# A new front for the scan layer of a two-layer perceiver kernel: input blocks in the cross-attention, step sizes by a stacked rounded product, first taps on ScalarE, other banks for folds

## The reference, cut to what matters

```python
def _L0_attn_ref(x, ...):                     # x: 16 x 64 x 256, after a layernorm
    x_b, res = split(x @ in_proj_w.T + in_proj_b, 2)          # 512 channels each
    xc = depthwise_conv(x_b, conv_w, 4 taps, causal) + conv_b
    x_b = silu(xc)
    delta, b, c = split(x_b @ x_proj_w.T, [16, 32])           # 16 + 16 + 16 columns
    delta = softplus(delta @ dt_proj_w.T + dt_proj_b)
    a = -exp(A_log)
    h = exp(delta * a) * h + delta * b * x_b  # 64 steps in time, 16 states a channel
    y = sum over states(h * c) + x_b * D_param
    return (y * silu(res)) @ out_proj_w.T + out_proj_b
```

## Time and profile before

| | us |
|---|---|
| median of 3 runs | 684.99 |
| lowest and highest | 683.14, 686.74 |
| the profiled execution | 687.29 |
| its span on the core | 685.6 |
| TensorE busy | 619.4 |
| VectorE busy | 471.8 |
| ScalarE busy | 366.0 |
| GpSimd busy | 223.2 |

### The profile page before, as it was taken

How to read it: one execution, slowest core, us unless ns; L and a number is a source line. 1 busy time by engine, 2 the same in 40 slices (tenths; PEclk the granted TensorE clock), 3 DMA queues, 4 the chain that set the end, 5 groups by cost and what they waited for, 6 DMA issues and landing times. The chain is left out here.

```text
span 685.6 us, 11634 instructions
## 1 busy us (share of the span) xinstructions
PE 619.4 (90%) x4414; PEld 461.1 (67%) x4414; DVE 471.8 (69%) x804; ACT 366.0 (53%) x679; POOL 223.2 (33%) x180
## 2 busy tenths in 40 slices
PE   3998999998998777887878899999999999999997
PEld 2453555554335666776767888887877767889897
DVE  5122333345857989999999746678987778777554
ACT  2310111123549898999999742433566456455342
POOL 2000000000003999999989200034553021232000
PEclk9998999999999999999999999999999999999999
DMA  8999999882821232232331000000100022120000
GB/s 309 394 336 420 418 420 419 319 316 77 231 83 43 74 108 98 93 120 97 106 111 62 1 1 1 16 1 17 34 3 3 1 63 77 47 62 1 32 1 32
DMA packets 31071, 86.48 MB, mean 126 GB/s; under 512 B 7900, under 2 KB 19576, under 8 KB 28840
## 3 DMA queue, kind: packets, MB, share of 16 engines
q1 hardware_dynamic: 30456, 85.28, 34.3%
q10 hardware_dynamic: 560, 0.46, 0.3%
HBM read 83.50 MB, written 1.11 MB: 123 GB/s over the span
## 5 line engine op out<-in xcount | busy, mean ns | idle before, releaser
L692 POOL TENSOR_TENSOR dbu<-du,bs 128x1024 f32<-128x1024 f32 x63 | 148.8, 2414 | 212.3 <-DVE du L884 209.5
L906 DVE TENSOR_TENSOR_SCAN w_in<-hS,dbu 128x1024 f32<-128x1024 f32 x42 | 94.7, 2273 | 0.1
L784 ACT ACTIVATE weighed<-T,CT 128x256 f32<-128x256 f32 x220 | 90.8, 536 | 3.4 <-PE T L988 3.1
L773 ACT ACTIVATE hS<-delta,negA 128x504 f32<-128x504 f32 x128 | 86.9, 751 | 7.6 <-DVE xn L906 5.4
L1002 PE MATMUL Y<-ident,weighed 128*128 128x128 f32 x512 | 67.7, 275 | 0.1
L988 PE MATMUL T<-ident,w_in 128*128 128x128 f32 x336 | 46.6, 282 | 22.3 <-ACT weighed L784 13.6
L1002 PEld LDWEIGHTS Y<-ident,weighed 128*128 128x128 f32 x512 | 58.7, 142 | 0.8 <-DVE sres L927 0.3
L988 PEld LDWEIGHTS T<-ident,w_in 128*128 128x128 f32 x336 | 36.7, 142 | 32.7 <-DVE w_in L906 30.7
L906 DVE TENSOR_TENSOR_SCAN xn<-hS,dbu 128x1024 f32<-128x1024 f32 x22 | 50.1, 2278 | 5.6 <-issue 4.7
L258 PE MATMUL S<-cT,qkT 128*64 128x512 f32 (+1 forms) x256 | 47.7, 527 | 2.8 <-DMA cT<-in_ctxT 2.8
L270 PE MATMUL O<-cN,pT 128*64 128x256 f32 x384 | 46.7, 385 | 0.0
(11 more groups left out here) (416 smaller groups left out, 1315.9 us busy)
## 6 DMA issues: line engine op xcount, KB each, us to landing
cT<-in_ctxT SPq DMA_DIRECT2D x8, 3202.0 KB, 15.5
cN<-in_ctx SPq DMA_DIRECT2D x8, 3072.0 KB, 14.4
bs<-b_rows SPq DMA_DIRECT2D x32, 512.0 KB, 3.5
raw_w<-in_w SPq DMA_DIRECT2D x16, 256.0 KB, 2.8
w<-in_w SPq DMA_DIRECT2D x7, 256.0 KB, 8.3
vs<-vx SPq DMA_DIRECT2D x8, 136.0 KB, 2.3
x<-in_x SPq DMA_DIRECT2D x2, 512.0 KB, 6.0
cR<-in_ctx SPq DMA_DIRECT2D x1, 1024.0 KB, 32.3
```

Of the source, the lines that this page charges most:

```text
L692: e.tensor_tensor(dbu[s % NB][:, :, :], half(m.du, s // DS), row, ALU.mult).then_inc(s_bu, 1)
L773: i = e.activation(by_batch(A[s % 2][:, j * HALF:(j + 1) * HALF]), by_batch(m.delta[:, c, h * HALF:(h + 1) * HALF]), ACT.Exp, scale=m.negA ...
L784: i = e.activation(weighed[s % 2][:, q * Q:(q + 1) * Q], T[:, q * Q:(q + 1) * Q], ACT.Copy, scale=c_of(s, q))
L906: e.tensor_tensor_scan(S[s % NS], A[s % 2][:, :], dbu[s % NB][:, :, :].rearrange("p c n -> p (c n)"), 0.0, ALU.mult, ALU.add).then_inc(s_h, 1)
```

## The change

- The cross-attention's end makes four input blocks, not one. Block 0 stands ahead of the last fold of `on`, block 1 ahead of the last output projection, 2 and 3 around the last two folds of normed tokens. ScalarE moves all four out there.
- The first tap is ScalarE's (`first_tap`), into four buffers and not two; VectorE does three taps.
- `x_proj` writes 128 rows: the 16 rows of delta three times (rows 0, 32, 64) and b and c at 96. ScalarE rounds 80 of them to fp32r (`large_part`), VectorE writes what the rounding left to rows 32 on (`small_part`). The weights are prepared alike by GpSimd (`w_dt3`), so that one product of 80 rows of rounded operands gives the three larger terms. Four banks serve for it, not two.
- GpSimd, idle in the front before, copies `w_xp`'s columns, prepares `w_dt3` and adds the output bias `outb` to `k.x` (128x2048), which VectorE did in the last step.
- Softplus goes in three parts: the first two channel blocks before `absolute` 3 to 7, the others on ScalarE after the first decays. Max(z, 0) plus logarithm of the second half moves from GpSimd to VectorE (steps 2 and 3), those of blocks 1 to 3 of the first half to GpSimd.
- The products of layer 1's weights use Y where they used A; ScalarE copies their results out, after the decays of step 2. TensorE makes D times u for the first unit after the first fold, and step 1 isn't weighed by VectorE any more, nor step 0.
- b goes to memory and back for each half by itself. `w_dt` is loaded three times; two clears at the program's start grow, and `own_head`, which nothing read, goes.

```diff
-    def begin_scan_layer():
-        e.wait_ge(k.s_wi, 16)
-        e.wait_ge(s_xT, 2)
-        project_in(e, k, 0, bank[2]).then_inc(s_in, 1)
+    def begin_scan_layer(n):
+
+        if n == 0:
+            e.wait_ge(k.s_wi, 16)
+            e.wait_ge(s_xT, 2)
+        project_in(e, k, n, bank[(n + 2) % 4]).then_inc(s_in, 1)
...
                 turn(i - 1, g)
+        if i > TILES:
+            begin_scan_layer(0)
         if i >= 2:
             weighted(i - 2)
+        if i > TILES:
+            begin_scan_layer(1)
...
-    begin_scan_layer()
+    begin_scan_layer(2)
     turn_normed(2)
+    begin_scan_layer(3)
     turn_normed(3)
...
+    def keep_block(n):
+
+        e.wait_ge(s_in, n + 1)
+        if n < 2:
+            e.wait_ge(s_tn, n + 1)
+        e.activation(xb(k, n), bank[(n + 2) % 4], ACT.Identity, bias=col(k, "inb", n)).then_inc(s_xb, 1)
+
+    keep_block(0)
+    keep_block(1)
     root(2)
-    e.wait_ge(s_in, 1)
-    e.wait_ge(s_tn, 2)
-    e.activation(xb(k, 0), bank[2], ACT.Identity, bias=col(k, "inb", 0)).then_inc(s_xb, 1)
-    for n in (2, 3):
-        move_normed(n)
+    keep_block(2)
+    move_normed(2)
+    keep_block(3)
+    move_normed(3)
...
+with ExitStack() as front:
+    sbf, _, _ = tools(nc, front)
+    dtr3 = sbf("dtr3", [DT_ROWS, TOK], F32R)
+    w_dt3 = sbf("w_dt3", [DT_ROWS, DI], F32R)
...
-acc4 = [weighed[1][:, r * HALF:(r + 1) * HALF].rearrange("p (b l) -> p b l", l=L) for r in range(2)]
+acc4 = [weighed[r // 2][:, r % 2 * HALF:(r % 2 + 1) * HALF].rearrange("p (b l) -> p b l", l=L) for r in range(4)]
...
-kTb = dbu[2][:, :, :].rearrange("p c n -> p (c n)")[:, 0:KD * (D + 1)].rearrange("p (c n) -> p c n", c=KD)
-qk, qk_at = A[1].rearrange("p (j n) -> p j n", j=KD), HALF // 2 + 8
+kTb = k.xz[:, :, :].rearrange("p c n -> p (c n)")[:, 0:KD * (D + 1)].rearrange("p (c n) -> p c n", c=KD)
+qk, qk_at = Y.rearrange("p (j n) -> p j n", j=KD), HALF // 2 + 8
-xq, dq = ([a[:, i * HALF:(i + 1) * HALF] for i in range(2)] for a in A)
+xq = [a[:, 0:HALF] for a in A]
+dq = [A[i % 2][:, (1 - i // 2) * HALF:(2 - i // 2) * HALF] for i in range(4)]
...
-    return s % 16 in (0, 1, 3, 5, 7, 9, 11, 13, 15)
+    return s > 1 and s % 16 in (0, 1, 3, 5, 7, 9, 11, 13, 15)
...
+    e.wait_ge(k.s_w2, k.n_w2)
+    for r in DT_AT[1:]:
+        i = e.tensor_copy(k.w_xp[:, :, r:r + DTR], k.w_xp[:, :, 0:DTR])
+    i.then_inc(s_ws, 1)
+    e.tensor_copy(w_dt3[:, :], k.w_dt[0:DT_ROWS, :]).then_inc(s_ws, 1)
+    e.wait_ge(s_ws, 2)
+    low = slice(DT_AT[2], DT_ROWS)
+    e.tensor_tensor(w_dt3[low, :], k.w_dt[low, :], w_dt3[low, :].bitcast(F32), ALU.subtract).then_inc(s_ws, 1)
+    e.wait_ge(s_ws, 3)
+    e.wait_ge(k.s_rows, 16)
+    e.tensor_tensor(k.x[:, :, :], k.x[:, :, :],
+                    rowvec(k, "outb").unsqueeze(1).to_broadcast([P, TILES, D]), ALU.add).then_inc(s_xo, 1)
     for s in range(1, STEPS):
-        if s in (3, 6):
-            steps_by_input(0, s // 3 + 1)
-        if s in (9, 12, 21, 24):
-            add_parts((9, 12, 21, 24).index(s))
-        if s in (15, 18, 34, 37):
-            steps_by_input(1, (15, 18, 34, 37).index(s))
         if s == 1:
-            e.wait_ge(s_du, 2)
+            add_parts(1)
+            steps_by_input(0, 1)
+        if s in (4, 8):
+            add_parts(2 + (s - 4) // 4)
+        if s in (6, 10):
+            steps_by_input(0, 2 + (s - 6) // 4)
+        if s in (18, 22, 26, 30):
+            steps_by_input(1, (18, 22, 26, 30).index(s))
+        if s == 1:
+            e.wait_ge(s_du, 1)
+            e.wait_ge(s_dup, 2)
+            e.wait_ge(s_fp, pe_at["dt", 7])
...
+    def first_tap(n):
+
+        c = n % CH
+        if n >= CH:
+            e.wait_ge(s_fa, ac_at["xb", n])
+            e.wait_ge(s_fa, ac_at["u", n - 4])
+        e.activation(acc4[n % 4][:, :, :], xb(k, n).rearrange("p (b l) -> p b l", l=L), ACT.Identity,
+                     scale=col(k, "convw", c * KC + KC - 1), bias=col(k, "convb", c)).then_inc(s_fa, 1)
...
+    def large_part(h):
+
+        e.wait_ge(s_fp, pe_at["xj", h])
+        e.activation(dtr3[:, h * HALF:(h + 1) * HALF], xq[h][0:DT_ROWS, :], ACT.Copy).then_inc(s_fa, 1)
...
+    parts = (halves[0][:, 0:2, :], halves[0][:, 2:4, :], halves[1])
+
+    def exponential(g):
+        e.wait_ge(s_fa, ac_at["abs", (1, 3, 7)[g]])
+        e.activation(parts[g], parts[g], ACT.Exp, scale=-1.0).then_inc(s_fa, 1)
+
+    def logarithm(g):
+        e.wait_ge(s_fa, ac_at["exp", g])
+        e.activation(parts[g], parts[g], ACT.Ln, bias=1.0).then_inc(s_fa, 1)
+
+    first_tap(0)
+    first_tap(1)
+    keep_block(4)
+    first_tap(2)
     silu_u(0)
...
+    for n in range(3):
+        absolute(n)
+    large_part(1)
+    keep_rows(1)
+    e.preload_act_table_set("natural_log_exp_and_others")
+    exponential(0)
+    logarithm(0)
+    for n in range(3, 2 * CH):
+        absolute(n)
-    e.activation(m.delta[:, :, :], m.delta[:, :, :], ACT.Exp, scale=-1.0).then_inc(s_fa, 1)
-    e.wait_ge(s_fa, ac_at["exp", 0])
-    for part in (halves[0][:, 0:2, :], halves[0][:, 2:4, :], halves[1]):
-        e.activation(part, part, ACT.Ln, bias=1.0).then_inc(s_fa, 1)
+    e.wait_ge(s_fa, ac_at["exp", 3])
     e.mul(m.negA[:, :, :].rearrange("p c n -> p (c n)"), expA[:, :], -1.0).then_inc(s_fa, 1)
...
     decays(0)
+    e.wait_ge(s_fp, pe_at["vo", 0])
+    e.activation(vT, T[:, HALF:2 * HALF], ACT.Copy).then_inc(s_vo, 1)
+    exponential(1)
+    exponential(2)
+    decays(1)
+    logarithm(1)
+    logarithm(2)
+    decays(2)
+    e.wait_ge(s_fp, pe_at["b", 0])
+    e.activation(k.w5[0][:, :, :], qk[:, :, 0:D], ACT.Copy)
+    e.activation(k.w5v[:, :, D + 2], qk[:, :, D], ACT.Copy)
+    e.activation(k.bq5[:, :], Y[:, qk_at:qk_at + KD], ACT.Copy)
+    e.activation(k.btq[:, 2:3], Y[:, qk_at + KD:qk_at + KD + 1], ACT.Copy).then_inc(s_qt, 1)
     e.wait_ge(s_fp, pe_at["vo", 1])
     e.activation(k.wfq[0:1, :], spare[0:1, 0:D], ACT.Copy)
     e.activation(k.w5v[:, :, 0:D], T[:, HALF:2 * HALF].rearrange("p (c n) -> p c n", c=KD), ACT.Copy).then_inc(s_vo, 1)
-    decays(1)
     e.wait_ge(s_ct, 1)
     for s in range(STEPS):
-        if s + 2 < STEPS:
+        if 0 < s < STEPS - 2:
             decays(s + 2)
...
-        if n:
-            e.wait_ge(s_fa, ac_at["xb", n])
-        if n >= 2:
-            e.wait_ge(s_fa, ac_at["u", n - 2])
-        for j in range(KC):
+        e.wait_ge(s_fa, ac_at["tap", n])
+        for j in range(1, KC):
             tap = col(k, "convw", c * KC + KC - 1 - j)
-            if j == 0:
-                e.tensor_scalar(acc4[r][:, :, :], x, tap, col(k, "convb", c), ALU.mult, ALU.add).then_inc(s_cv, 1)
-            else:
-                e.wait_ge(s_cv, 4 * n + j)
-                e.scalar_tensor_tensor(acc4[r][:, :, j:L], x[:, :, 0:L - j], tap, acc4[r][:, :, j:L],
-                                       ALU.mult, ALU.add).then_inc(s_cv, 1)
-
-    def keep_rows(h):
+            if j > 1:
+                e.wait_ge(s_cv, 3 * n + j - 1)
+            e.scalar_tensor_tensor(acc4[r][:, :, j:L], x[:, :, 0:L - j], tap, acc4[r][:, :, j:L],
+                                   ALU.mult, ALU.add).then_inc(s_cv, 1)
+    def small_part(h):
+
         hs = slice(h * HALF, (h + 1) * HALF)
-        e.wait_ge(s_fp, pe_at["xj", h])
-        e.tensor_copy(dtr[:, hs], xq[h][0:DTR, :])
-        e.tensor_copy(m.bc[32:64, hs], xq[h][32:64, :]).then_inc(s_xe, 1)
+        at = slice(DT_AT[1], DT_AT[1] + DTR)
+        e.wait_ge(s_fa, ac_at["hi", h])
+        e.tensor_tensor(dtr3[at, hs], xq[h][at, :], dtr3[at, hs].bitcast(F32), ALU.subtract).then_inc(s_lo, 1)
...
-    for n in range(6):
+    for n in range(7):
         convolve(n)
-    keep_rows(0)
-    convolve(6)
-    positive(0)
-    positive(1)
+    small_part(0)
     convolve(7)
-    positive(2)
-    positive(3)
-    keep_rows(1)
     for c in range(CH):
         i = e.tensor_scalar(m.diagD[:, c, :], k.ident[:, :], col(k, "dpar", c), None, ALU.mult)
     i.then_inc(s_dg, 1)
-    for n in range(CH, 2 * CH):
+    for n in range(3):
         positive(n)
+    small_part(1)
...
-    e.tensor_copy(CT[:, :, :], T[:, 0:TILES * 2 * DS].rearrange("p (t n) -> p t n", n=2 * DS)).then_inc(s_ct, 1)
-    for c in range(2):
-        add_parts(c)
-    for c in range(2):
-        e.wait_ge(s_dl, c + 1)
-        e.tensor_tensor(m.du[:, c, 0:HALF], m.delta[:, c, 0:HALF], m.u[:, c, 0:HALF], ALU.mult).then_inc(s_du, 1)
-    e.wait_ge(s_du, 2)
+    e.tensor_copy(kTb[:, :, 0:D], Y[:, HALF:2 * HALF].rearrange("p (c n) -> p c n", c=KD)).then_inc(s_qt, 1)
+    positive(3)
+    raw_gate(6)
+    positive(4)
+    add_parts(0, 0)
+    e.wait_ge(s_dl, 1)
+    e.tensor_tensor(m.du[:, 0, 0:HALF], m.delta[:, 0, 0:HALF], m.u[:, 0, 0:HALF], ALU.mult).then_inc(s_du, 1)
+    for n in range(5, 2 * CH):
+        positive(n)
+    for r in range(2):
+        e.wait_ge(s_fa, ac_at["abs", 2 * CH - 2 + r])
+        e.wait_ge(s_rz, 2 * CH - 1 + r)
+        zeros(r)
+    e.wait_ge(s_fp, pe_at["dt", 7])
+    e.wait_ge(s_du, 1)
+    e.wait_ge(s_dup, 2)
```

(65 more changed lines are left out.)

174 lines of the change are left out of this document (84 added, 90 removed).

## The result

The kernel before took 684.65 us (median of 7 runs, 683.1 to 686.8), the changed kernel 690.32 (7 runs, 689.2 to 692.9). The ratio is 1.0096, with a 95% interval of 1.0076 to 1.0117: 0.96% slower. The forecast was 690.4. One execution of a kernel of experiment 10 (727.3 us) and two of the kernel before beside it (799.4 and 805.6) ran at a much lower granted clock (0.74 to 0.85 against 0.98 and more) and are in no median or count of this document. The profiled execution of the changed kernel took 692.55, with a span of 690.8; that of before took 687.29, with a span of 685.6.

What follows compares the result with a forecast made beforehand. Front: TensorE, VectorE and ScalarE hand work to each other; steps: GpSimd bounds long, later VectorE and ScalarE. Terms +5.4 + 2.4 - 2.35 = +5.45 on the 684.99 median gave 690.4 us; forecast range 687.5 to 692.5.

Steps and rivals of the forecast that it cites:

- X: End of the second x_proj in each kernel; forecast 5.4 us later than before.
- X to scan 10: From the second x_proj's end to scan 10: X+51.8 instead of X+49.4, +2.4 us, bounds -1.5 to +4.
- End of the cross-attention: More input blocks on TensorE there end the stage later, with nothing hiding it: +3.8, taken as 3.9 us.
- GpSimd beside the taps: In the front, VectorE's two-input taps wait for whole GpSimd operations: +6.0 us, bounds 0 and 7.5.
- First x_proj: In the front, after the fourth block's taps and silu: starts at 186.6 us, before 178.51.
- The clock: TensorE's idle time before the first x_proj brings one fall to 1.2 GHz: 1.0 us taken, of 0 to 1.7.
- Behind scan 10: Scans 10 to 34: GpSimd, with four operations more, stops being the bound and the pace quickens: -2.35 us.
- The bias gone from VectorE's last step: Last step: removing the bias add gains 0, since out_proj on TensorE is the path there.
- The sum at scan 63: All terms together: +5.4 + 2.4 - 2.35 = +5.45 us.
- Rival 1: GpSimd's long operation lets VectorE in, so 4.7 of the 6.0 us beside the taps go: 685 us, chance 0.18.
- Rival 2: Shared access costs nothing in the front's taps or the later additions: -5.0, 680 us, chance 0.14.
- rival 3: Steps don't recover behind scan 10 and the clock falls fully: 693.5 us, chance 0.18 including beyond.

Runs made afterwards that it cites:

- experiment 10: Experiment 9's kernel with idle TensorE products filling two waits, then two products in the second, then a third wait too: 681.61, 681.78, 681.30 us (0.9943, 0.9968, 0.9936).
- Experiment 8: Changed kernel with two input blocks in the cross-attention instead of four, the other two first on TensorE in the layer: 688.03 us, ratio 1.0049.
- experiment 1: Changed kernel with the output bias added by VectorE in the last step again, not by GpSimd at the layer's head: 685.12 us, ratio 1.0030.
- experiment 3: Kernel before with only the output bias moved from VectorE's last step to GpSimd at the layer's head: 691.00 us, ratio 1.0103.
- experiment 7: Changed kernel with two idle block products on TensorE in its wait before the first x_proj: 690.60 us, ratio 1.0073.
- experiment 6: Changed kernel with the second half's four additions moved from VectorE to GpSimd at steps 12, 14, 20 and 24: 690.82 us, ratio 1.0086.
- experiment 9: Changed kernel with the bias on VectorE in the last step and the second half's additions on GpSimd at steps 12, 14, 34, 38: 683.19 us, ratio 0.9976.
- experiment 4: Kernel before plus a GpSimd copy of the residual's 2048 columns onto themselves at the layer's head: 688.34 us in one execution.

## Why the forecast came out

The direction, the size and the main cause stand, and the terms up to X and from X to scan 10 were off in opposite directions (-0.8 and +0.6). That the forecast of 690.4 and the median of 690.32 agree to 0.1 is luck: the seven executions alone spread over 3.6 us.

- **End of the cross-attention**, +3.9: 9.8 for 6.2, +3.6. The size held; the reason held in part. Experiment 8 shows that the two blocks behind the output projection cost 1.5 together and otherwise fill a wait; the rest is then left to the two ahead of it, which no run took out.
- **GpSimd beside the taps**, +6.0: 5.1 (7.29 from the first tap to the end of the third, for 2.2). The bias cost 4.1 of it (experiment 1), as the alternation by whole instructions has it. I had assumed that the first tap waits for the cast, and it did not (0.74). The Trainium skill, "SBUF — State Buffer", section "Who interferes with whom", has the rule that I had worked out from the earlier trace rows: the pair of ports that VectorE and GpSimd share is an exclusive lock, and a VectorE instruction with two SBUF inputs contends for it with a GpSimd instruction that reads SBUF. That whoever issues first holds it for the whole instruction, while the other one stands still, the section says of VectorE's modes that use both pairs of ports. The trace agrees, and shows it for two inputs too, at 4.86 us for one tap.
- **First x_proj**: I had 186.6 for a cross-attention as in before's profile. Less the 1.96 by which it was shorter it would be 184.6; it was 183.3.
- **The clock**, 1.0 of 0 to 1.7: it was the upper end. The x_proj took 1.8 more, and experiments 3 and 7 show the same figure (1.7) coming with the wait and going with it. The forecast had one fall; after had two more behind X, from 207.5 to 217.8 and from 238.2 to 245.1, for which the sum has no term.
- **X**, +5.4: 41.9 for 37.3, +4.6.
- **X to scan 10**, +2.4: +3.0. The chain was right where it mattered: the first fold at X+24.4 (forecast X+24.4), scans 4 and 5 at X+33.4 and X+39.4 (X+33.6, X+39.8). Decays 3 ended at X+27.8 (forecast X+27.6), and scan 3 ran from X+27.9 to X+30.2, so that the forecast's "scan 3 at X+30" fits its end. The exponentials and logarithms behind the first decays are six of the eight blocks, as the forecast counted them, not half as the section on the change says. Of the pairs I had 3.6 each, they took 3.43 and 3.41, and their worth on the path is 5.2 in all (experiment 6).
- **Behind scan 10**, -2.35: -2.45.
- **The bias gone from VectorE's last step**, 0: 0 (experiment 1).

The sum at scan 63 was +5.45, and the traces give +5.2. Rival 1, that a long operation of GpSimd lets VectorE in, has fallen: it predicted 685 by taps of 0.74. Rival 2 gave 680 if sharing cost nothing, and its premise is false: sharing cost 5.1 beside the taps. What it gave the rest of the change, -5.0, was too much: without the bias in the front, the time is that of before (experiment 1), and without the additions on VectorE as well it is 1.6 below it (experiment 9). Of rival 3 the fall of the clock came to its full size and the missing recovery did not. What I had not seen is how much hangs on one instruction: it alone makes a loss of 1% (experiment 3), and without it the rest of the new front is not to be told from the kernel before (1.0030, experiment 1), with 3.6 lost at the end of the cross-attention against what is gained behind.

## What to carry to other kernels

An idle engine is not a free one: before work goes to GpSimd, look at what VectorE does in that stretch, and put long instructions of GpSimd where VectorE reads from PSUM or waits. A wait of TensorE can cost twice, once as a wait and once as the products behind it at half the clock: here waits of 3.9 to 4.0 us before the first x_proj did (experiments 3 and 7), and in experiment 10 the stretches at 1.2 GHz left the front as its waits were filled. But not each wait of that length was followed by one, and the filling is worth 0.4% at most here. An edit that frees time ahead of a queue that is nearly full (here GpSimd's) pays only as far as the work moved is spread over the steps where the queue has slack.

## What the hardware showed that I had not expected

- VectorE's multiplication of one SBUF tensor by a column (128x512, float32) waits for GpSimd as the taps with two inputs do: 4.86 us instead of 0.55 beside an addition, 2.15 beside a copy. I had expected it of two inputs only. The Trainium skill, "SBUF — State Buffer", section "Who interferes with whom", names multiplications by a scalar among those that can contend, in a mode that uses both pairs of ports. The trace agrees that it contends; in which mode it ran, no run here shows.
- The order of the starts in the profile does not tell who gets the access: that multiplication began at 163.42, GpSimd's addition at 163.49, and VectorE waited for its end. By that section of the Trainium skill the first to issue has it; if this holds here, a start in the profile is not the moment at which it is decided.
- GpSimd's addition of 2048 columns took 4.51 to 4.82, its copy of as many 1.89, VectorE's addition 2.27.
- TensorE's clock fell to 1.2 GHz in or behind waits of 1.5 to 4.0 us in a front and in first steps in which it was otherwise busy, and stayed low for 3.4 to 17.1 us; a wait of 2.92 (experiment 1) and waits of 1.63 and 1.50 (experiment 4) were followed by no such stretch at once. The Trainium skill, "TensorE: Matmul & The Clock Gate", section "Why this matters for your kernels", advises against idle gaps between bursts of products, and names longer ones than the shortest here. The measurement goes further: in experiment 10 a gap of 2.10 was followed by such a stretch and one of 0.39 was not.
